# A two-layer transformer kernel: another order of work and of loads in its head, and filler products for the first scores

## The reference, cut to what matters

```python
xn = layernorm(x)
# first layer: 16 heads of 8, keys and values in a latent of 64
k_eff = (W_dq.T @ W_uq.T @ W_uk) ;  v_eff = (W_uv.T @ W_o.T)
q = xn @ W_dq.T @ W_uq.T ;  c_kv = xn @ W_dkv.T
attn = softmax(causal(q k_eff c_kv / sqrt(8))) ;  s = attn c_kv v_eff
# beside it: 8 experts of 64, the best 2 by (cosine + linear) logits
h = gelu(xn @ w1 + b1) ;  g = sum_e gate_e (h @ w2 + b2)
x = x + s * silu(g)
# second layer: a linear-attention recurrence over the tokens
# (W -= 0.01 (W k - v) k^T, y = W q) and a feed-forward with sign(weight)
x = x + (xn2 + y) * silu(xn2 @ sign(weight).T)
```

## Time and profile before

| | us |
|---|---|
| median of 3 runs | 709.38 |
| lowest and highest | 709.02, 711.78 |
| the profiled execution itself | 706.64 |
| its span, first to last instruction | 704.20 |
| last weight table ready, start of the first transposes of sequence 0 | 12.35 |
| first row maximum on DVE starts | 39.38 |
| last row maximum of the first round ends | 78.77 |
| first exponential of the second round starts | 83.01 |

### The profile page before, as it was taken

One profiled execution on the slowest core, in us unless ns is written; L12 is line 12 of the kernel. 1 busy time (PEld: TensorE's weight loads), 2 busy tenths in 40 slices (PEclk: granted clock), 3 DMA queues, 4 the chain that ended last, 5 costly groups with the idle time before them and its releaser, 6 DMA issues.

```text
span 704.2 us, 16715 instructions
## 1 busy us (share of the span) xinstructions
PE 603.2 (86%) x6886; PEld 389.3 (55%) x6886; DVE 419.5 (60%) x1033; ACT 363.6 (52%) x742; POOL 171.6 (24%) x322
## 2 busy tenths in 40 slices
PE   4487898999897999898998989798998998896864
PEld 2143464566564755566564756575565665553653
DVE  1366666666758476857667575947676665414341
ACT  3200646845664556645674465645673667473310
POOL 4373103222314111412223121511231202212111
PEclk9999999999998999999998999899999999998675
DMA  2663001610142004310251014300330000000000
GB/s 75 154 174 86 1 8 32 156 40 2 54 115 66 8 10 114 86 36 2 76 128 33 7 31 105 99 8 10 103 94 23 2 9 16 23 1 3 1 17 15
DMA packets 28870, 35.59 MB, mean 51 GB/s; under 512 B 3932, under 2 KB 25243, under 8 KB 27643
## 3 DMA queue, kind: packets, MB, share of 16 engines
q1 hardware_dynamic: 28794, 34.53, 19.2%
HBM read 24.46 MB, written 9.96 MB: 49 GB/s over the span
## 4 chain that ended last, share of the span: by engine, by line
PE 58%; DVE 18%; issue 8%; ACT 7%; POOL 6%; DMA 1%; SPq 1%; POOLq 0%; DVEq 0%; ACTq 0%
PE ps_v L843 8%; PE ps_s L824 8%; PE ps_e L809 6%; DVE cand L1313 4%; PE ps_a L771 4%; PE ps_a L759 4%; PE ps_e L806 3%; PE ps_s L827 3%; DVE second L1258 3%; PE ps_a L734 2%; PE ps_c L908 2%; DVE stats L1244 2%; DVE hid L1297 1%; PE ps_c L982 1%; PE ps_c L890 1%
## 5 line engine op out<-in xcount | busy, mean ns | idle before, releaser
L1313 DVE TENSOR_REDUCE cand<-ps_s 128x4 f32<-128x512 f32 (+1 forms) x320 | 213.0, 684 | 75.3 <-PE ps_s L827 54.6
L1118 ACT ACTIVATE prob<-ps_e 128x512 f32<-128x512 f32 x320 | 187.8, 596 | 106.5 <-PE ps_e L809 102.6
L824 PE MATMUL ps_s<-kst,qst 72*128 72x128 bf16 (+1 forms) x1024 | 132.8, 246 | 23.1 <-DVE cand L1313 22.5
L809 PE MATMUL ps_e<-qst,kst 75*128 75x384 bf16 (+3 forms) x512 | 124.0, 304 | 0.0
L824 PEld LDWEIGHTS ps_s<-kst,qst 72*128 72x128 bf16 x1024 | 76.1, 103 | 84.6 <-DVE cand L1313 55.3
L843 PE MATMUL ps_v<-prob,vaug 128*32 128x512 f32 (+3 forms) x1024 | 91.8, 456 | 0.0
L806 PE MATMUL ps_e<-identb,negmask 128*128 128x256 bf16 (+1 forms) x320 | 81.8, 256 | 10.9 <-ACT prob L1118 10.8
L809 PEld LDWEIGHTS ps_e<-qst,kst 75*128 75x128 bf16 x512 | 50.9, 99 | 18.6 <-issue 1.2
L827 PE MATMUL ps_s<-negmask,identb 128*128 128x512 bf16 x128 | 52.9, 413 | 0.0
L615 POOL CAST mparts<-nm 128x32 bf16<-128x32 f32 x16 | 3.4, 210 | 172.7 <-DVE nm L1320 172.7
L806 PEld LDWEIGHTS ps_e<-identb,negmask 128*128 128x128 bf16 x320 | 31.7, 99 | 22.2 <-ACT prob L1118 18.3
(11 more groups left out here) (315 smaller groups left out, 950.4 us busy)
## 6 DMA issues: line engine op xcount, KB each, us to landing
qst<-q_scratch SPq DMA_DIRECT2D x48, 192.0 KB
kst<-k_scratch SPq DMA_DIRECT2D x16, 576.0 KB
q_scratch<-qparts SPq DMA_DIRECT2D x24, 128.0 KB, 2.3
k_scratch<-kparts SPq DMA_DIRECT2D x24, 128.0 KB, 2.2
xn<-in_L_attn_x_dram SPq DMA_DIRECT2D x8, 256.0 KB, 3.1
x_res<-in_L_attn_x_dram SPq DMA_DIRECT2D x8, 256.0 KB, 2.9
out_dram<-second SPq DMA_DIRECT2D x7, 256.0 KB, 2.4
max_scratch<-mrow SPq DMA_DIRECT2D x16, 96.0 KB, 1.7
```

The source lines that it names most:

```text
L809: last = mm(ps_e[:, bank, at:at + TOK - P * j], k[0:SROWS, hd, tok(j)], q[0:SROWS, hd, P * j:TOK], start=False, stop=True, skip_group_chec ...
L824: last = mm(ps_s[:, bank, w * n:w * (n + 1)], q[0:PAIRS, hd, tok(i)], k[0:PAIRS, hd, keys[0]:keys[1]], start=(n == 0), stop=True, skip_gro ...
L1118: af(prob[:, u, :], ps_e[:, u % 2, :], ACT.Exp).then_inc(S["e_emptied"], 1)
L1313: vec.tensor_reduce(cand[:, i, h0:h0 + FILLS * (len(hds) - 1) + 1:FILLS, S_SLOT[u]], ps_s[:, u % 2, :].rearrange("p (a c) -> p a c", a=len ...
```

## The change

All of it lies in the head and in the first round; the plan of the other rounds is the same, and the numbers of fillings are now counted from the written order.

- SP loads x, then the two matrices for q (semaphore `q_loaded`), then the two for k (`k_loaded`), then the small ones. The ten other loads are issued by ACT, as the first thing in its list.
- The weight products are reduced to one transpose and four products for `w_q` and `w_k`; those for `w_v` move into `prepare`.
- k of sequence 0 goes to the bank `ps_v` and not to `ps_a`, and DVE, not POOL, makes its second and third part.
- `constants` of POOL come behind the power of sequence 0. `masks` is split: the second part, `masks2`, comes in the first round.
- The order of the head is written out in `HEAD`. Logits, gates, their transpose, the four expert products and the Gelu of sequence 0 stand in it, among the pieces of sequence 1. The first round has the plan `FIRST_PLAN`.
- PE gets filler products (`keep_busy`): bf16, 128x512, into a half of `ps_e` that nothing reads. There are three ahead of the first wait, then one or two behind the weight products, two behind the transposes of sequences 0 and 1, seven in `prepare`, two behind each expert product of sequence 0, eight at the end of the head, and one behind each of the 40 score units of the first round.

```diff
-HEAD = ("load_x", "ln1_stats", "ln1_rstd", "ln1_norm", "xnt", "q", "k")
+HEAD = [("weights", None), ("ln1_stats", 0), ("ln1_rstd", 0), ("constants", None), ("ln1_norm", 0), ("xnt", 0), ("q", 0), ("k", 0),
+        ("rn_first", 0), ("load_x", 1), ("stacks0", 0), ("stacks1", 0), ("prepare", None), ("logits", 0), ("ln1_stats", 1), ("ln1_rstd", 1),
+        ("h0", 0), ("ln1_norm", 1), ("xnt", 1), ("gates", 0), ("q", 1), ("h1", 0), ("k", 1), ("stacks0", 1), ("stacks1", 1), ("h2", 0),
+        ("h3", 0), ("gt", 0), ("gelu", 0), ("masks", None), ("busy", None)]
+FIRST_PLAN = {(2, 0): ["m_parts0"], (2, 4): ["m_rows0"], (2, 5): ["masks2"], (3, 2): ["v"], (4, 0): ["m_parts1"]}
...
-        first_loads = [
-            (nat["uq"][:, :], W_uq), (nat["o"][:, :], W_o), (nat["dq"][:, :], W_dq), (nat["dkv"][:, :], W_dkv), (nat["uk"][:, :], W_uk),
-            (nat["uv"][:, :], W_uv), (nat["cent"][:, :], cent_in)]
+        q_loads = [(nat["uq"][:, :], W_uq), (nat["dq"][:, :], W_dq)]
+        k_loads = [(nat["uk"][:, :], W_uk), (nat["dkv"][:, :], W_dkv)]
         loads = [
...
+            def keep_busy(n):
+
+                for _ in range(n):
+                    mm(ps_e[:, 1, :].rearrange("p (a c) -> p a c", c=P), identb[:, :], bcast(identb[:, :], 1, 4), start=True, stop=True,
+                       skip_group_check=True)
+
+            def weights():
+                keep_busy(3)
+                pe.wait_ge(S["q_loaded"], Q_LOADED)
+                prep(tr(ps_s[0:QL, 0, 0:P], nat["uq"][:, :], ident[:, :]))
+                keep_busy(1)
+                ready(1)
+                prep(mm(ps_s[:, 1, 0:P], uqT[:, :], nat["dq"][:, :], start=True, stop=True))
+                prep(mm(ps_e[:, 0, 0:P], nat["dq"][:, :], uqT[:, :], start=True, stop=True))
+                keep_busy(1)
+                ready(2)
+                pe.wait_ge(S["k_loaded"], K_LOADED)
+                prep(mm(ps_c0[0:KVL, 0:P], nat["uk"][:, :], wqeT[:, :], start=True, stop=True))
+                keep_busy(2)
+                ready(4)
+                prep(mm(ps_c1[:, 0:P], nat["dkv"][:, :], keffT[:, :], start=True, stop=True))
+                keep_busy(2)
+                ready(5)
 
             def prepare():
                 pe.wait_ge(S["const_ready"], 4)
                 pe.wait_ge(S["loaded"], LOADED)
...
+                keep_busy(4)
+                ready(PREP_RW)
+                prep(tr(ps_s[:, 0, 0:2 * EXPERTS], rw[:, :], ident[0:2 * EXPERTS, 0:2 * EXPERTS]))
+                prep(mm(ps_s[0:KVL, 1, 0:P], nat["uv"][:, :], oT[:, :], start=True, stop=True))
+                keep_busy(3)
+                ready(PREP_OUT - 1)
+                prep(mm(ps_e[:, 0, 0:P], nat["dkv"][:, :], veff[:, :], start=True, stop=True))
...
+                if b.c < 2:
+                    keep_busy(2)
 
             def qk(b, n):
-                a_fill(b, A_Q + n)
-                mm(ps_a[:, :], (w_q, w_k)[n][:, :], xnT[b.parity][:, :], start=True, stop=True).then_inc(S["a_filled"], 1)
+                bank = ps_a
+                if b.c == 0 and n == 1:
+                    bank = ps_v
+                else:
+                    a_fill(b, ("q", "k")[n])
+                mm(bank[:, :], (w_q, w_k)[n][:, :], xnT[b.parity][:, :], start=True, stop=True).then_inc(S["a_filled"], 1)
...
             def h(b, c):
...
+                if b.c == 0:
+                    keep_busy(2)
...
                 if cur is not None:
                     e_unit(cur, grp, u)
+                else:
+                    keep_busy(1)
...
-            act.wait_ge(S["first_loaded"], FIRST_LOADED)
-            af(cent_sq[:, :], nat["cent"][:, :], ACT.Square, accum_out=cent_ss[:, :]).then_inc(S["cent_ss_ready"], 1)
+            for dst, src in loads:
+                act.dma_start(dst, src).then_inc(S["loaded"], 16)
```

More of the change, by code:

```diff
@@ L159, in head_of, with iteration, schedule, numbers @@
     return FH * (grp // FILLS) + FILLS * hh + grp % FILLS
[L162 to L172, removed]
+def iteration(second, nxt, cur, prev, older, plan=PLAN):
+    for step in range(1 + max(at[0] for at in plan)):
+        for u in range(UNITS):
+            if step < GROUPS:
+                yield "unit", (cur, nxt, step, u)
+            for name in plan.get((step, u), []):
+                if name in PLAN_COMMON:
+                    yield name, ()
+                    continue
+                of = second if name in PLAN_SECOND else nxt if name in PLAN_NEXT else \
+                    cur if name in PLAN_CURRENT or name.startswith("last:") else older if name in PLAN_OLDER else prev
+                name = name.removeprefix("last:").removeprefix("prev:")
+                if of is not None:
+                    yield name, (of, step) if name in ("pv0", "pv1") else (of, step - 1) if name in ("pv2", "yt") else (of,)
+def schedule():
+    seqs = [Seq(c) for c in range(SEQUENCES)]
+    for name, c in HEAD:
+        yield name, () if c is None else (seqs[c],)
+    yield from iteration(None, seqs[0], None, None, None, plan=FIRST_PLAN)
+    yield "settle", ()
+    for t in range(2, SEQUENCES):
+        yield from iteration(*(seqs[t - behind] if t >= behind else None for behind in range(5)))
+    yield from iteration(None, *seqs[:SEQUENCES - 5:-1])
+    yield from iteration(None, None, *seqs[:SEQUENCES - 4:-1], plan=LAST_PLAN)
+def numbers(pieces, last_apart=False):
+    table, count = {}, [0, 0]
+    for piece, at in schedule():
+        if piece in pieces:
+            own = int(last_apart and at[0].c == SEQUENCES - 1)
+            table[at[0].c, piece] = count[own]
+            count[own] += 1
+    return table
+A_NUMBER = numbers(A_PIECES)
+C0_NUMBER, C1_NUMBER = numbers(C0_PIECES, True), numbers(C1_PIECES, True)
 def after(eng, sem, value):
@@ L353, in bcast, with run @@
             return ap.to_broadcast(shape)
[L355 to L396, removed]
+        def run(pieces):
+            for name, at in schedule():
+                if name in pieces:
+                    pieces[name](*at)
         x_view = x_in.rearrange("b (i p) d -> b p i d", p=P)
@@ L885, in c_vk @@
                 r, o = second_layer(b)
-                for bank, fill, filled, n in ((r.ps_c0, c0_fill, "c0_filled", C0_VK), (r.ps_c1, c1_fill, "c1_filled", C1_VK)):
+                for bank, fill, filled, n in ((r.ps_c0, c0_fill, "c0_filled", "c_vk"), (r.ps_c1, c1_fill, "c1_filled", "c_vk")):
                     fill(b, n)
@@ L1011, in _ @@
                 pieces[f"c_y{c}"] = lambda b, c=c: c_y(b, c)
-            run(pe, pieces, unit, prepare, settle)
+            run(pieces | {"unit": unit, "weights": weights, "prepare": prepare, "settle": settle, "busy": lambda: keep_busy(8)})
         @block.scalar
@@ L1190, in _ @@
             pieces[f"lev_d{IN_SQUARE}"] = lev_d
-            run(act, pieces, unit, prepare)
+            run(pieces | {"unit": unit, "weights": weights, "prepare": prepare})
         @block.vector
@@ L1433, in _ @@
                 pieces[f"lev_a{lv}"] = lambda b, lv=lv: lev_a(b, lv)
-            run(dve, pieces, unit, prepare, settle)
-PREP_OUT = 18
+            run(pieces | {"unit": unit, "prepare": prepare, "settle": settle})
+PREP_OUT, PREP_RW = 18, 14
 S_UNIT = [(i, (P * i, P * i + P), (0, 1, 2, 3)) for i in range(4)] + [
```

311 lines of the change are left out of this document (153 added, 158 removed).

## The result

The changed kernel takes 703.57 us (median of 5 runs, 702.07 to 704.33) against 709.02 for the kernel before (median of 5, 707.09 to 711.78). The ratio is 0.9917, with a 95% interval of 0.9890 to 0.9944: 0.8% faster, 5.5 us. The forecast was a median of 708.0. Both profiled executions lie at an edge of their runs: the one before took 706.64, which is under all five, and the one after 704.33 (span 702.6), the highest of its five. So the two traces differ by only 2.3 us in all, and 5.5 is to be had from the medians alone.

The account below looks back on a forecast made before the run. PE is busy 86% of the span, but the head is a serial chain, with PE at its lower clock until about 71.8 us. Terms +11.8 - 10.2 - 3.0 = -1.4 us gave a median of 708.0, range 700 to 713.

Parts of the forecast that it names:

- the case that I had likeliest: Whole kernel: median 708.0, own range 705.5 to 711, chance 0.45; a change under 0.5% counts as none, 0.44.
- Faster by more: Whole kernel: faster by more than 0.5% (3.5 us), chance 0.37.
- rival 1: Head: the higher clock holds, 31 us for 39.5, total 699.5 (chance 0.08); for about half the chain, 704 (0.27).
- The start of the transposes: Start of head: first copy on ACT at 6.6 us, first transposes at 11.7 against 12.35 before.
- The chain of the head: First transposes to first row maximum: 39.5 us, low clock until h2; first maximum at 51.2, 11.8 later than before.
- The first round: 40 maxima at 0.70, plus 0.25 and 0.95: 29.2 us against 39.4, saving 10.2; DVE hides the filler.
- The 0.95 for `v`: First round: making `v` (1.16 us of PE) delays one score unit by about 0.95 us.
- The start of the second round: After the last maximum: ACT is free and the Exp table loaded early, saving 3.0 us.
- Sum: Whole kernel: +11.8 - 10.2 - 3.0 = -1.4 us, profiled execution 705.2, median 708.0.
- The later rounds: Rounds after the head and first round: shift as they are; four short low-clock spells may move, 2 us either way.
- Rival 2: First score units: clock still low, filler makes PE the bound, +5.2 us, 714.6; chance 0.20.
- its two largest terms: First maximum 11.8 us later (head), and 10.2 us saved in the first round.

Follow-up runs that it names:

- the kernel with the tail's filler: Changed kernel plus one filler product behind each piece of the last levels, in the last two sequences: 700.38 us, ratio 0.9865.
- The held head: Changed kernel with more filler where PE waited in the head (14 for 4, 11 for 2, new 9 and 5): 698.35 us, ratio 0.9833.
- the kernel with the constants whole: Changed kernel with sequence 0's first-layer work back in the first round and POOL's constants in one piece ahead of it: 708.16 us, ratio 0.9981.

## Why the prediction was right and wrong

The direction was right and the range of 700 to 713 holds the result, but the case that I had likeliest (705.5 to 711, and a change too small to tell from none, 0.44) was not the one that came. Faster by more had 0.37. The measured chain from the transposes to the first maximum is 35.3 us, in the middle between my 31 (clock up) and 39.5 to 42 (down): rival 1 in its half form, to which I had given 0.27 and a time of 704. The measured time is 703.57. That these two agree so well is in part luck: the first round came out 2.5 us shorter than my term and the later rounds gave back 5.5 in the traces, neither of which is in the 704.

Step by step, in the profiled executions:

- **The start of the transposes** (step: 11.7). It was 12.76. The table load came behind the issues, at 6.33, and the copy at 7.62, past the 7.3 that I had as the upper end: ten issues on ACT ended at 6.30, not at 6.05. Between the ends I had chosen 6.6, for no reason that a row gave. The Trainium skill's figure for load and drain ("ScalarE: Activation LUTs", What ACT_TABLE_LOAD costs) would, as an estimate, have put the copy at about 9.0 behind this load. The copy began 0.01 us after the load ended, so for this first load the measurement goes against the drain. With the loads on SP, the transposes come 2.8 earlier: this part, which looked like the change's gift to the head, costs it 0.4 as it stands.
- **The chain of the head** (step: 39.5 with the low clock until h2). This is the step that failed, by 4.2. I had rightly seen that PE waits 3 us for the centroids and that the clock falls: it fell at 21.7. But it had been up from 14.9 before that (q of sequence 0 took 1.40, where a pair at the low clock takes 1.96), and it rose at 35.3, in q of sequence 1, not with h2: h1's pair took 1.13 at 37.23, for which I had 1.95. Of the waits that I had named only the first was as long as I said: PE waited 1.34 for the scaling of sequence 1 and 1.40 for q's rest. Up to h1 my list at the low clock was good to 0.7 (25.2 from the start of the transposes, measured 24.5); from h1 to the first maximum it had 17.0 and the trace has 10.9, where I had taken off only 2.7 for the clock. Why the clock rose at 35.3 and not later, I did not settle; the kernel with the tail's filler, with the same head, had it up over 4 us sooner. The held head got to 46.02, 33.2 from the start of its transposes, against my 31.
- **The first round** (step: 29.2). It was 26.7. I had taken a maximum at 0.70 from a run of seven and the real rate is 0.65 over 21, which makes 40 come to 25.9; pairs in the earlier trace rows stood at 1.28 and 1.29 and said so. The 0.95 for `v` held: DVE waits 0.86 once, ahead of the 34th maximum, while PE makes `v`. 25.9 and 0.86 make up the round; the 0.25 for the reduction of the first half's maxima shows no delay of its own. `masks2` was hidden, as said. That DVE hides the filler holds at the high clock: PE is busy 26.60 of 27.00 us there, and DVE 25.46.
- **The start of the second round** (step: −3.0). 4.89 became 1.74: −3.15. This step held.
- **Sum.** First maximum +8.7, round −12.7, start −3.15: the third exponential unit is 7.1 earlier (83.66 to 76.53), where I had 1.4.
- **The later rounds** (step: they shift as they are, 2 us either way). They do not. In these traces x1 of sequence 0 is 5.2 earlier, and the end 1.6. Windows of the changed kernel around the first loss:

```profile
103.70:107.00 3.30, 1.62 (x18) 1.30 (x16) 1.81 (x7) 1.74 (x3) 1.33 (x3) 1.00 0.06 14
107.00:110.40 3.40, 3.39 (x18) 2.19 (x22) 2.53 (x5) 2.05 (x9) 0.00 (x0) 0.54 0.10 27
```

PE is busy for half of the first, and in the next the granted clock is 0.54. A spell costs 1.9 us (78.08 against 76.2, before and after alike). The changed execution has spells at 107.0, 216.3, 369.9, 448.4, 526.9 and 591.7 ahead of the last sequence's end, the one before at 222.0, 375.6, 454.1 and 597.5. The one at 107.0 and the one at 597.5 are half as long as the others. Two more spells are about 3.8 of the 5.5 us that this pair of executions gave back between the third exponential unit and the end. The rest lies in the last stretch, which is 61.53 long against 60.35, and in shares of spells. Since spells differ between two executions of one kernel, too, the medians carry the comparison. What decides in which rounds a spell falls, I did not settle.

**Rival 2**, the clock still low at the scores, did come in the kernel without filler: 32.0 for the round, and slower than before by 5 us. I had it in the wrong place. The eight fillers and the one per unit are what keeps it away.

**Which part brings the gain.** My sum treated the move of sequence 0's work as the change's centre, and its two largest terms, +11.8 and −10.2, are mostly that work leaving one place for the other. The runs show it as a wash (1.8 us, not clear of nothing). What pays is a pair. Filler alone gives nothing (1.0003), since PE then waits for POOL's constants. The new order without filler loses 0.7%. With both, the clock up and POOL's constants out of the way, it is 0.5% with the move undone and 0.8% with the move, where DVE's maxima run with the one break for `v`. Three things stay open. The filler and the split of the constants alone, on the kernel before, were not run. The bank for k of sequence 0 and DVE's part in it were in every variant and never undone; the kernel with the constants whole differs from the filler on the kernel before by these, by the weights and loads and by the head's other fillers, 708.16 against 710.42 with intervals that overlap. And no run shows why a spell falls in one execution and not in another.

## What to carry to other kernels

In the first round filler paid only once nothing else held the stage: first take away what PE waits for, then fill, and measure each alone and both together, because here the singles were 0 (eight fillers and one per unit) and −5 us and the pair +5.5. Before a trace's difference is put down to an edit, see what the same stage does in a trace where it was not edited: here that was up to 1.8 us in the head and 2 in the tail. When a kernel issues its first loads from an engine that also computes, put the issues on that engine's list of work with their real price, about 0.55 us each here. And price a move of work as two terms in one line, out of one stage and into the other, before looking at anything else: their difference is the whole effect.

## What the runs showed of the hardware

- The granted-clock column reads 1.00 from the start of a trace until the first change on record, whether PE is fast or slow: in the kernel before, products ran at half rate until 71.8 us under it. Durations of one known shape tell the clock there.
- Five rounds of the changed kernel have a wait of PE of 2.03 us or 2.04, ending at 215.08, 293.15, 369.38, 447.46 and 525.52. Four of them have a fall of the clock shortly behind it (the one at 293.15 has none), and such a spell costs 1.9 us in a round of 76.2, in a kernel where PE is busy 88%. Six products in the wait gave 4 us over the kernel.
- Ten DMA issues on ACT took 5.5 us (0.80 to 6.30), and the table load stands behind them, not at the start as in the kernel before. No time shows between the load's end and ACT's next instruction, here (7.61 and 7.62) or at 83.00 in the kernel before.
